# Self attention with rotary embedding: the rotation's partner rows by a VectorE shuffle instead of a second projection, two picks by ScalarE, a new list of slots

## The reference

```
x1 = ln(x, norm1) * (1 + sc_msa) + sh_msa          # sc, sh, g from cond @ adaLN_W, per sequence
q, k, v = split(x1 @ qkv_W)                         # self attention, 128 keys
q, k = rope(q), rope(k)      # t * cos + rot(t) * sin, rot(t) = concat(-t2, t1) over halves of each head's 8
x  = x + g_msa * (softmax(mask(q k^T / sqrt(8))) v) @ attn_out_W
x  = x + g_x   * cross(ln(x, normc) ..., ctx)       # 77 keys, cq_W, ck_W, cv_W, co_W
x  = x + g_mlp * (gelu(ln(x, norm2) ... @ W1 + b1) @ W2 + b2)
out = x + attention(ada_ln(x), ada_ln(ctx)) @ Wp + bp   # layer 2, 77 keys
```

## Time and profile before

| | us |
|---|---|
| median of three runs | 1152.88 |
| profiled execution, its own time | 1151.61 |
| its span | 1149.8 |
| PE busy | 1055.0 (92%) |
| DVE busy | 824.8 (72%) |
| ACT busy | 846.6 (74%) |
| POOL busy | 852.6 (74%) |

### The profile page before, as it was taken

One profiled execution on the slowest core, in us unless ns is written; L12 is line 12 of the kernel. 1 busy time (PEld: TensorE's weight loads), 2 busy tenths in 40 slices (PEclk: granted clock), 3 DMA queues, 4 the chain that ended last, 5 costly groups with the idle time before them and its releaser, 6 DMA issues.

```text
span 1149.8 us, 42336 instructions
## 1 busy us (share of the span) xinstructions
PE 1055.0 (92%) x16226; PEld 600.8 (52%) x16226; DVE 824.8 (72%) x2195; ACT 846.6 (74%) x1527; POOL 852.6 (74%) x1804
## 2 busy tenths in 40 slices
PE   5679999999998799999999888999999999999987
PEld 5435555555554355555555554444444566666665
...
GB/s 160 187 126 114 112 101 132 114 100 108 116 95 91 87 97 108 113 112 119 115 111 108 120 9 1 1 0 4 56 28 68 124 127 131 125 138 118 139 93 33
DMA packets 165018, 110.40 MB, mean 96 GB/s; under 512 B 42553, under 2 KB 164434, under 8 KB 164818
## 3 DMA queue, kind: packets, MB, share of 16 engines
...
...
## 4 chain that ended last, share of the span: by engine, by line
PE 54%; POOL 19%; ACT 12%; issue 5%; DVE 5%; ACTq 1%; SPq 1%; DMA 1%; POOLq 0%; DVEq 0%
PE ps_po L539 10%; PE ps_pj L437 7%; ACT p L816 6%; PE ps_nat L490 6%; PE ps_st L518 6%; PE ps_pj L415 5%; PE ps_st L551 4%; PE ps_po L560 4%; PE ps_pj L420 3%; POOL parts L919 3%; PE ps_nat L475 3%; POOL ht L943 3%; POOL ht L938 2%; PE ps_pj L428 2%; DVE negmax L623 2%
## 5 line engine op out<-in xcount | busy, mean ns | idle before, releaser
L623 DVE TENSOR_REDUCE negmax<-ps_nat 128x8 f32<-128x616 f32 (+1 forms) x384 | 359.7, 937 | 63.4 <-PE ps_nat L490 55.0
L816 ACT ACTIVATE p<-ps_st 128x1024 f32<-128x1024 f32 (+1 forms) x256 | 260.9, 1019 | 152.3 <-PE ps_st L518 150.3
L539 PE MATMUL ps_po<-p,vz 77*32 77x128 f32 (+1 forms) x6144 | 253.3, 283 | 4.6 <-DVE mt L631 1.9
L539 PEld LDWEIGHTS ps_po<-p,vz 77*32 77x32 f32 (+1 forms) x6144 | 149.3, 111 | 44.0 <-issue 12.3
L816 ACT ACTIVATE p<-ps_st,key_bias 77x1024 f32<-77x1024 f32 x128 | 141.4, 1105 | 33.9 <-PE ps_st L518 33.8
L518 PE MATMUL ps_st<-stacks 64*77 64x128 bf16 (+1 forms) x3072 | 155.1, 222 | 11.4 <-ACT p L816 5.0
L900 POOL TENSOR_TENSOR ot<-vv,den 128x128 f32<-128x128 f32 x192 | 87.4, 455 | 98.8 <-ACT den L804 89.4
L490 PEld LDWEIGHTS ps_nat<-stacks 64*128 64x128 bf16 x3072 | 78.1, 97 | 126.4 <-issue 113.8
L490 PE MATMUL ps_nat<-stacks 64*128 64x77 bf16 (+1 forms) x3072 | 133.9, 209 | 5.3 <-DVE negmax L623 3.5
L518 PEld LDWEIGHTS ps_st<-stacks 64*77 64x77 bf16 (+1 forms) x3072 | 104.6, 110 | 23.9 <-ACT p L816 20.8
L911 POOL TENSOR_TENSOR whole<-whole,parts 128x512 f32<-128x512 f32 x96 | 98.6, 1027 | 4.6 <-ACT parts L751 4.5
...
## 6 DMA issues: line engine op xcount, KB each, us to landing
stacks<-parts SPq DMA_DIRECT2D x512, 128.0 KB, 3.2
...
```

The lines of the kernel that those rows point to most:

```text
L539: m = t.matmul(c.ps_po[step % 2][32 * g:32 * g + 32, S * p:S * p + S], c.vz[0:nk, i % 2, step % G, g, at:at + 32], c.p[0:nk, hh, S * g:S * ...
L623: v.tensor_reduce(c.negmax[:, step % 2, :].rearrange("p (h q g) -> p h q g", h=2, q=2)[:, :, p, :], c.nat_pair[:].rearrange("p (h n) -> p ...
L816: a.activation(c.p[0:nk, 2 * p:2 * p + 2, :].rearrange("p h n -> p (h n)"), c.st_pair[0:nk, :], ACT.Exp, bias=bias).then_inc(exped, 1)
```

## The change

1. `wrot` and the products qr and kr are gone. `take` multiplies the q (or k) bank by the cosine table into `part` and by the sine table into a new tile `spare`, and a VectorE `stream_shuffle` moves `spare`'s partner rows (row r ^ 4) to the second half of `part`. The sine table is itself shuffled once in the setup, so that each product has the partner's factor. `turn` waits for the shuffle (rotated).
2. In self attention the two picks of `read_out` are ScalarE activations (`begin_picks`), at the start of the odd slot, ahead of the exponential.
3. The self attention list: q in 8i - 21, k in 8i - 19, v in 8i - 4, c in 8i - 31 (i >= 1), m in 8i - 26 (i >= 1), o in 8i + 15. GpSimd's `apply_norm` stays in 8i - 22.
4. VectorE reads late products at the end of the slot throughout.
5. The norms of groups 0, 1, 2 are applied by VectorE (`apply_first`), in the slots in which GpSimd did it.
6. ScalarE issues only the 16 DMAs of the first output weight, in slots -28, -27, -26 and -24; SyncE issues the other 32 in even slots 24 to 86 and the seven larger ones in odd slots 25 to 37. TensorE waits for these 39 in slot 100, and for the 16 in slot 8. The key masks move from slots 40 and 44 to 41 and 45.

```diff
@@ -146,17 +149,10 @@
             act.dma_start(c.cos[:], ins["cos"]).then_inc(tables, 16)
-            act.dma_start(c.sin[:], ins["sin"]).then_inc(tables, 16)
+            act.dma_start(c.sin_in[:], ins["sin"]).then_inc(tables, 16)
             act.dma_start(c.wqkv[:], ins["L0_xcond_qkv_W"]).then_inc(wqkv, 16)
             a.activation(c.cond_t[:, 1, :], c.cond_t[:, 0, :], ACT.Exp, scale=-1.0).then_inc(silu_e, 1)
-            act.wait_ge(wqkv, 16)
-            for x in range(2):
-                src = c.wqkv[:, D * x:D * x + D].rearrange("p (h t e) -> p h t e", t=2, e=4)
-                dst = c.wrot[:, x, :].rearrange("p (h t e) -> p h t e", t=2, e=4)
-                for t in range(2):
-                    a.activation(dst[:, :, t, :], src[:, :, 1 - t, :], ACT.Copy)
@@ -188,6 +185,7 @@
 UNITS = GROUPS * PER
+SELF_STEPS = NG * G
 AHEAD = 6
@@ -222,16 +220,16 @@
             b, u = head_of(i), slot_of(PER * i)
-            for kind, r in ((("q", 0), ("qr", 1), ("k", 2), ("kr", 3)) if i < NG else (("q", -1), ("k", 1))):
+            for kind, r in (("q", -1), ("k", 1)):
                 self.add(self.late, b + r, (kind, i))
             if i < NG:
-                self.norm(("n", i), b - 6, 3 if i >= 1 else 0)
+                self.norm(("n", i), b - 6, 5 if i >= 1 else 0, 2 if i >= 1 else 0)
             elif 2 * NG <= i < 2 * NG + 4:
                 self.norm(("n", i), b - 13)
-            self.add(self.late, u - (6 if i < NG else 4), ("v", i))
-            first, second = (u + 12, u + 12) if i == GROUPS - 1 else (u + 14, u + 15) if i >= 2 * NG else (u + 15, u + 15) if i >= NG - 2 else (u + 17, u + 17)
+            self.add(self.late, u - 4, ("v", i))
+            first, second = (u + 12, u + 12) if i == GROUPS - 1 else (u + 14, u + 15) if i >= 2 * NG else (u + 15, u + 15)
             self.add(self.late, first, ("o", i))
@@ -285,12 +283,12 @@
-    def norm(self, which, s, sooner=0):
+    def norm(self, which, s, sooner=0, mean_sooner=0):
         self.add(self.late, s - sooner, ("c", which))
-        self.add(self.late, s + 2 + wait, ("m", which))
+        self.add(self.late, s + 2 + wait - mean_sooner, ("m", which))
         self.add(self.pool_norm, s + 4 + wait, which)
@@ -357,6 +356,8 @@
     norm_of = lambda which: {"n": (c.xt, NT), "mlp": (c.xt, NT), "ctx": (c.ct, NC)}[which[0]]
+    first_norms = [("n", i) for i in range(3)]
+    picks_until = lambda step: step if step <= SELF_STEPS else SELF_STEPS + 3 * (step - SELF_STEPS)
     mlp_group = lambda slot: ((slot - MLP_SLOT) // 2, (slot - MLP_SLOT) % 2)
@@ -587,7 +588,9 @@
                 if slot == 8:
-                    pe.wait_ge(weights_here, 16 * (3 * 16 + 7))
+                    pe.wait_ge(out_weights_here, 16 * 16)
+                if slot == NG * PER - LEAD - 8:
+                    pe.wait_ge(weights_here, 16 * (2 * 16 + 7))
                 for job in plan.late.get(slot, []):
@@ -601,13 +604,14 @@
                 if a == 0:
-                    r = len(kind) - 1
                     if 2 * i + x > 0:
                         dve.wait_ge(turned, 2 * i + x)
-                    table = ((c.cosq, c.sinq), (c.cos, c.sin))[x][r]
-                    v.tensor_tensor(c.part[:, r, :].rearrange("p (r n) -> p r n", n=64),
-                                    bank[:].rearrange("p (r n) -> p r n", n=64),
-                                    table[:].unsqueeze(1).broadcast_to([128, 8, 64]), ALU.mult).then_inc(taken, 1)
+                    blocks = lambda tile: tile.rearrange("p (r n) -> p r n", n=64)
+                    for table, dst in zip(((c.cosq, c.sinq), (c.cos, c.sin))[x], (c.part[:, 0, :], c.spare[:])):
+                        m = v.tensor_tensor(blocks(dst), blocks(bank[:]), table[:].unsqueeze(1).broadcast_to([128, 8, 64]), ALU.mult)
+                    m.then_inc(taken, 1)
+                    dve.wait_ge(taken, plan.taken[job])
+                    v.stream_shuffle(c.part[:, 1, :], c.spare[:], PARTNER_ROWS).then_inc(rotated, 1)
                 else:
@@ -639,13 +643,17 @@
                 first, second = bank[:, 0:S], bank[:, S:2 * S]
-                v.tensor_scalar(c.dd[:, here, :], second, low, None, ALU.mult).then_inc(picked, 1)
-                v.tensor_scalar(c.vv[:, here, :], second, up, None, ALU.mult).then_inc(picked, 1)
-                dve.wait_ge(picked, 3 * step + 1)
+                if step < SELF_STEPS:
+                    dve.wait_ge(begun, 2 * step + 2)
+                else:
+                    v.tensor_scalar(c.dd[:, here, :], second, low, None, ALU.mult).then_inc(picked, 1)
+                    v.tensor_scalar(c.vv[:, here, :], second, up, None, ALU.mult).then_inc(picked, 1)
+                    dve.wait_ge(picked, picks_until(step) + 1)
                 v.scalar_tensor_tensor(out=c.dd[:, here, :], in0=first, scalar=up, in1=c.dd[:, here, :], op0=ALU.mult, op1=ALU.add).then_inc(picked, 1)
-                dve.wait_ge(picked, 3 * step + 2)
+                if step >= SELF_STEPS:
+                    dve.wait_ge(picked, picks_until(step) + 2)
                 v.scalar_tensor_tensor(out=c.vv[:, here, :], in0=first, scalar=low, in1=c.vv[:, here, :], op0=ALU.mult, op1=ALU.add).then_inc(po_read, 1)
-                dve.wait_ge(picked, 3 * step + 3)
+                dve.wait_ge(picked, picks_until(step + 1))
                 v.stream_shuffle(c.den[:, here, :], c.dd[:, here, :], DEN_ROWS).then_inc(den_here, 1)
@@ -708,13 +716,24 @@
+            def apply_first(i):
+                dve.wait_ge(rooted, i + 1)
+                v.tensor_tensor(ht(i), c.xc[:, i, :], c.nrm[:, i, :], ALU.mult).then_inc(multiplied, 1)
+                dve.wait_ge(multiplied, i + 1)
+                for b in range(G):
+                    n = G * i + b
+                    part = ht(i)[:, S * b:S * b + S]
+                    m = v.tensor_scalar(part, part, c.mod[:, 1, n:n + 1], c.mod[:, 0, n:n + 1], ALU.mult, ALU.add)
+                m.then_inc(applied, 1)
                     keep_x(load_slot[slot])
-                in_self = slot < NG * PER + PER
+                for which in plan.pool_norm.get(slot, []):
+                    if which in first_norms:
+                        apply_first(which[1])
                 coming = plan.dve_jobs.get(slot, [])
-                for job in coming if in_self else []:
-                    read(job)
                 g, second = mlp_group(slot - 4)
@@ -726,7 +745,7 @@
                     set_key_row(key_slots[slot])
-                for job in [] if in_self else coming:
+                for job in coming:
                     read(job)
@@ -795,6 +814,16 @@
+            def begin_picks(step):
+                act.wait_ge(pv_done, 2 * step + 2)
+                if step >= 2:
+                    act.wait_ge(out_ready, step - 1)
+                    act.wait_ge(den_here, step - 1)
+                second, here = c.ps_po[step % 2][:, S:2 * S], step % 2
+                a.activation(c.dd[:, here, :], second, ACT.Copy, scale=c.lower[:, 0:1]).then_inc(begun, 1)
+                a.activation(c.vv[:, here, :], second, ACT.Copy, scale=c.lower[:, 1:2]).then_inc(begun, 1)
@@ -921,6 +942,9 @@
                 k, w = plan.norms[which], norm_of(which)[1]
+                if k == len(first_norms):
+                    pool.wait_ge(multiplied, k)
+                    pool.wait_ge(applied, k)
                 if name == "n":
@@ -971,7 +995,8 @@
                 for which in plan.pool_norm.get(slot, []):
-                    apply_norm(which)
+                    if which not in first_norms:
+                        apply_norm(which)
                 for which, i, x in at_slot.get(slot, []):
```

More of the change, by code:

```diff
@@ L31 @@
 DEN_ROWS = [r ^ HD for r in range(32)]
+PARTNER_ROWS = [r ^ (HD // 2) for r in range(32)]
 VEC_ROW = {"L0_xcond_adaLN_b": 0, "L1_xcond_bss_q": 9, "L1_xcond_bss_kv": 11, "L0_xcond_norm1_w": 13,
@@ L182, in _ @@
                     mm.then_inc(made, 1)
+            pe.wait_ge(wqkv, 16)
             pe.wait_ge(ready, 1)
@@ L305, in by_dve @@
     def by_dve(self, job):
-        return job[0] in ("q", "qr", "k", "kr", "o") or job[0] == "c" and not self.copied_by_act(job[1])
+        return job[0] in ("q", "k", "o") or job[0] == "c" and not self.copied_by_act(job[1])
     @staticmethod
@@ L837, in keep_ctx, with bring_out_weights @@
                 a.activation(c.ct[:, NC * i:NC * i + NC], c.ps_nat[i % 2][:, 0:NC], ACT.Copy).then_inc(kept_c, 1)
-            def bring_out_weights(n, g):
-                rows = ins[("L0_xcond_attn_out_W", "L0_xcond_co_W", "L1_xcond_Wp")[n]].rearrange("(p g a e) n -> g a p e n", p=2, g=4, a=2)
+            def bring_out_weights(g):
+                rows = ins["L0_xcond_attn_out_W"].rearrange("(p g a e) n -> g a p e n", p=2, g=4, a=2)
                 for a2 in range(2):
@@ L844, in bring_out_weights @@
                         at = 32 * g + 16 * a2 + HD * p
-                        act.dma_start(c.wo[at:at + HD, n, :], rows[g, a2, p]).then_inc(weights_here, 16)
-            def bring_weights():
```

(42 more changed lines are left out.)

13 lines of the change are left out of this document (8 added, 5 removed).

## The result

The kernel after took 1171.85 us (median of 4 runs, 1169.26 to 1177.95), the kernel before 1152.89 on the same chip: ratio 1.0187, 95% interval 1.0156 to 1.0217. It is slower, as forecast (1162.5); whether the loss is over or under 2% the interval leaves open. The loss is 19.0 us, 7 more than the sum's 11.6, and the time lies above both ranges (1155 to 1170, 1147 to 1170). The profiled execution took 1171.9 us, its span is 1170.1.

The account below looks back on a forecast made before the run. Self attention was taken as bound by chained waits with every engine loaded, TensorE nearly full. Start -5.4, steady groups +7.5, end +9.5 sum to +11.6 on 1151.6, 1163.2, written 1162.5; own range 1155 to 1170, 8 in 10 1147 to 1170.

Parts of the forecast that it names:

- The slot's ring: Self attention: the next masks wait through VectorE's maximum or ScalarE's exponential, so an emptied slot saves 0.4 us, not 1.06.
- the steady period: Steady self attention: a group of eight slots takes 22.0 us against 21.21, +7.5 us over about ten groups.
- The first masks: Before slot 0: with weight DMAs moved off ScalarE, the first score masks come near 58 instead of 61.76, -3.8 us.
- Slots -6 to 10: Run-up after the first masks: the third norm no longer holds TensorE, -1.6 us more, within a start step of -5.4.
- the lock: First three norms: VectorE and GpSimd lock each other out of SBUF, 1.3 us a norm; sum 3 us higher, not counted.
- The end: End of self attention: GpSimd's norms of groups 16 to 18 wait for the later v, +9.5 us (+1 to +15).
- (a): Rival, steady groups: VectorE's longer take is hidden, groups take 20.0 us, total about 1140; 11%.
- (b): Rival, self attention: each product dropped gives back the full 1.06 us, total 1120; 2%.
- (c): Rival: steady groups stay even and the gain before slot 0 pays for the end, 1149 to 1155; 19%.
- the low end of the take: Steady slots: VectorE's two products and shuffle take 1.5 us instead of 1.93, making the group 21.1 us.
- (d): Rival: everything serial, groups at 22.6 us or more, low clock after each stop, 1171 or more; 9%.
- the clock term: End of self attention: TensorE's clock falls after stops, about 2 us a stop; sum 4 us higher, kept for the range.

Follow-up runs that it names:

- e3: The kernel after with the take's shuffle one slot later, behind that slot's maximum and read-out: 1159.02 us, ratio 1.0050 to the kernel before.
- e7: The kernel after with the two picks of self attention done by VectorE again: 1170.93 us.
- e2: The kernel after with the first three norms applied by GpSimd again: 1174.01 us.
- e6: The kernel after with v of groups 13 to 15 back in 8i - 6, the late shuffle, and the first three norms by GpSimd: 1144.37 us.
- e4: The kernel before with only the later weights' DMAs moved to SyncE: 1144.48 us, ratio 0.9949 to the kernel before.
- e12: e10 with GpSimd's norms of groups 1 to 15 one slot sooner: 1173.70 us.
- e13: e10 with GpSimd's order mended (slot 102's sum before the norm, group 17's norm in slot 110) and q of group 2 a slot later: 1131.33 us.
- e15: e2 with the product q of group 2 one slot later: 1174.09 us.
- e1: The kernel after with v of groups 13 to 15 back in slot 8i - 6: 1158.74 us, ratio 1.0061 to the kernel before.
- e10: e6 with c, m and norm of groups 16 to 18 in other slots: 1140.79 us, ratio 0.9903 to the kernel before.
- e5: The kernel after with e1's and e3's edits together: 1143.39 us, ratio 0.9942 to the kernel before.

## Why the prediction was right or wrong, step by step

**The slot's ring and the steady period: right.** 22.0 was predicted, 21.97 measured. (Its four parts add to 22.03, 0.82 over 21.21; ten groups of that are the 8.2 us that came, where the prediction wrote 7.5.) The parts: take 1.93 against 1.94; slots 4 and 5 5.89 against 2.64 + 3.26 = 5.90; slots 6 and 7 5.89 against 5.90; slots 0 and 1 5.0 against 5.0; slots 2 and 3 5.25 against 5.16, with q waiting for GpSimd's scaling as said. Two of the pieces are shown by runs: the shuffle ahead of mt (e3) and the picks (e7). The new list and the reading at the end of the slot (points 3 and 4) were not run one by one; what each is worth by itself is not shown.

**The first masks: right** (58, 57.66). But kernels with the same code up to there had them at 55.5 to 57.7, so one profile settles this to a us or two.

**Slots -6 to 10: wrong by 6 us**, -1.6 predicted, +4.5 measured; with the first masks +0.4 in place of -5.4, outside the -10 to -1 given. Two things in it. The norms on VectorE were costed at 1.8 us "by VectorE's rows", which are rows of operations that read PSUM. Here they read and write SBUF: beside an idle GpSimd 0.69 and 1.12 for the four scalings, but beside its splits 1.40 and 3.72, and the next maximum queued behind. One of GpSimd's own copies stretches with them (1.07 us at 58.51, 0.61 at 46.70). A norm beside the splits took 5.1 us instead of the 1.8 of the sum, which is more than the 1.3 us set aside for a lock. The rule that the prediction set against the change, that of the Trainium skill's SBUF — State Buffer (Who interferes with whom), is an exclusive lock; the trace agrees in kind. The two casts of the earlier trace rows, though, do not show it as the prediction read them: GpSimd filled vz beside both, from 1.41 for 2.66 us and again from 4.13 for 1.65 us. e2 says that the lock alone decides little, since GpSimd's norm holds q up instead. The rest is the new order: with GpSimd's norms, a late shuffle and v early (e6) it still takes 45.0 where the old list with the same DMAs (e4) takes 40.3. Slots -1 to 1 hold 3.4 of these 4.7 us (9.9 against 6.5), first e4's, then e6's two stretches:

```profile
73.71:80.25 6.54, 5.46 (x103) 2.64 (x102) 5.25 (x7) 2.71 (x4) 5.90 (x10) 1.00 0.61 115
```
```profile
74.49:80.26 5.77, 2.58 (x49) 1.39 (x50) 4.56 (x8) 3.00 (x5) 4.34 (x8) 0.72 0.80 145
80.26:84.40 4.14, 4.14 (x50) 2.02 (x50) 1.23 (x1) 1.92 (x3) 3.09 (x7) 0.56 0.20 29
```

Where the old list had a product in slots -1 and 0, the new one has none, yet slot -1 is longer: 2.92 us instead of 2.09. TensorE stands in it for VectorE's maximum, which queues behind the take of k (itself 0.36 us behind GpSimd) and mt:

```profile
74.80 0.69 DVE L611 TENSOR_TENSOR part<-ps_pj,cos 128x512 f32<-128x512 f32 x1 [0.36 <-POOL whole L934]
75.41 0.68 DVE L611 TENSOR_TENSOR spare<-ps_pj,sin 128x512 f32<-128x512 f32 x1
76.01 0.21 DVE L640 COPY mt<-ps_po 128x128 bf16<-128x128 bf16 x1
76.14 1.22 DVE L632 TENSOR_REDUCE negmax<-ps_nat 128x8 f32<-128x1024 f32 x1
...
77.41 0.61 PE L476 MATMUL ps_nat<-rolled,eye_bf 32*32 32x512 bf16 x2 [2.17 <-DVE negmax L632]
```

Then the clock is down, 0.50 in slot 0 (2.85 us instead of 2.23) and 0.56 in slot 1, and slot 1, empty in e4, has c in e6: 4.14 us instead of 2.23. In the kernel after, the shuffle stands ahead of this maximum as well and slot -1 lasts 3.64; e3 shows that part, 2.91. The rest is read from the rows; no run moved this take or filled these slots, and e12, e13 and e15, which moved the norm or q, did not help. So it stays an explanation.

**The end: the mechanism right, the size wrong**, +9.5 predicted, +16.0 measured, just above its upper bound of +15. e1 gives 14.9 back with one line. GpSimd waited 3.91, 6.54 and 6.68 us for v, where 5 and more was forecast for each. The term of this wait was +14; the slots of the stops (100, 108, 116) grew by 11.4, and the products saved gave 6.2 instead of 4.5. What failed are two terms that the sum put at nothing. One is the clock: the prediction had it in its upper bound, at 2 us a stop, and left it out of the sum; the slots behind the stops (101, 109, 117) grew by 5.3, slot 101 alone from 3.41 to 6.18. The Trainium skill's TensorE: Matmul & The Clock Gate, Part 1, has the array at half its clock after idleness, and the trace bears it out with 0.50 over 6.18 us. The other is VectorE's part: TensorE waited for its reading or for mt in slots 93, 94 and 103, and these and slot 95, with the clock at 0.73 behind, grew by 5.5 us. Slot 94 grew by 2.6 for a reason that I had not looked for: emptying the slots of qr and kr changes which product shares a PSUM bank with which, so m of group 15 waited for VectorE's read of k; in e10, where c and m stand elsewhere, slot 94 is 2.60. Slot 103 is 4.28 with the whole take ahead of mt, 3.54 with the late shuffle (e5), 2.65 before.

**After slot 122** the work is nearly the same, and the profile after is 4.4 us shorter there. The profiles of the fifteen kernels of the experiments lie, for the same stretch, between 729.1 (e13) and 739.8 us (e10), so a difference between executions can be all of it; this stays open.

**Rivals.** (a) and (b) fell with the period. (c) needed the low end of the take. (d), 1171 or more, is the time that came, and of its two conditions the low clock after the stops came, the groups at 22.6 did not: they were at 22.0, and the missing 7 us lie in the run-up and the end. Had the sum kept the clock term and the lock at their own price, it would have been 4 + 3 us higher, 1169 to 1170. That would have been near by luck in part: e2 gets 1.5 us at most for the lock, and the shorter end after slot 122 hides 4.4 us that the other stretches lost.
